# Grouped convolution ahead of a windowed attention: unstacked convolution for the first two images, one transfer per 32 channels, and a reordered preparation stage

## The chip, the cores and the metric

One core of a Trainium2 chip runs the kernel. The metric is the time of one execution on the device in microseconds (us), lower is better. TensorE is the matrix engine (PE in the profile, PEld its weight loads), VectorE is DVE, ScalarE is ACT, GpSimd is POOL, and SyncE (SP) only issues transfers. ScalarE and GpSimd issue transfers too, so SPq and ACTq in a row mean the transfer-issuing side of those engines.

## The reference, cut to what matters

The input is 16 images of 28 x 28 positions and 128 channels, all in float32. Two residual blocks follow each other:

```python
x = x + conv3x3(group_norm(x), W)          # 32 groups of 4 channels, "SAME" padding
x = x + neighborhood_attention(group_norm(x), w_qkv, b_qkv, rpb, w_proj, b_proj)
```

`group_norm` takes its statistics over all positions of an image and 4 channels. The convolution has 32 groups of 4 channels, so an output channel reads only the 4 input channels of its group. The attention has 16 heads of 8 dimensions, each query looks at a 7 x 7 window of keys, and a learned table `rpb` of 13 x 13 entries per head is added to the logits by relative position.

## The kernel before, in words

Channels lie on the 128 partitions, positions along the free dimension. The program is written engine by engine, with the order on each engine written out by hand and semaphores between them. It has two stages.

**The preparation stage** (up to about 242 us) runs over 32 **slots** `h`, two per image, each for 14 of the 28 rows (392 positions) of image `m = h // 2`. It loads the images in natural layout, turns each to channels-on-partitions on TensorE (`turn_input`, L1336, seven 112 x 112 transposes, four in the first half of the slot and three in the second), keeps them by ScalarE (`keep_input`, L807) and takes their statistics on VectorE (`input_stats`, L1052). The statistics of four images at a time go through a chain of small steps on VectorE, TensorE and ScalarE (`CHAINS`, L379). VectorE writes the normalized image into a zero-bordered buffer `padded[m % 2]` (`pad_image`, L1107). Then the convolution of that image can run (`convolve`, L1365), in two forms:

- **Unstacked**, for image 0 only: nine matmuls per slot, one per tap of the 3 x 3 filter, each with a 128 x 128 weight `wconv` that is zero outside the 4 x 4 group blocks. The moving operand is `padded` itself, shifted by the tap. `wconv` is loaded by GpSimd's queue (L689) and masked by VectorE (L1246).
- **Stacked**, for images 1 to 15: for each block `t` of 32 channels three copies of the padded image, shifted by 0, 1 and 2 columns, are put on top of each other on 96 partitions. One matmul with a 96 x 32 weight `wstack` then handles three taps of 32 channels, and the four blocks `t` write four different quarters of the output partitions. A slot takes 3 filter rows x 4 blocks = 12 such matmuls. The copies are transfers from SBUF to SBUF (`copy_image`, L473), three per block, twelve per image: SyncE issues those of blocks 0 and 1, ScalarE those of blocks 2 and 3, in slot `2m - 2`, once `pad_image(m)` is done.

VectorE adds the convolution to the image (`add_conv`, L1110), and takes the statistics of the second norm (`output_stats`, L1116). Beside the convolution each slot prepares the attention. In slots 3 to 16 TensorE picks the position biases from the table, two **units** a slot, each 24 or 32 small matmuls (`pick_unit`, L1401), and VectorE keeps them in three additions each (`keep_unit`, L1140). In slots 17 to 24 two **patches** a slot are rounded by VectorE (`round_patch`, L1158, in the slot ahead), turned by TensorE (`turn_patch`, L1419) and placed by VectorE (`place_patches`, L1170). In slots 18 to 20 the first image is projected to keys, queries and values (`project_qkv`, L1391); ScalarE takes the results from PSUM (`keep_qkv`, L848). In slots 20, 22 and 24 SyncE stores them in parts to DRAM, in slot 25 it loads them back in the layout of the scores (`fill_queries`, `fill_keys`), and in slots 26 to 28 the first maxima are computed.

The order of a slot on TensorE is in L1523 to L1559: the small sums of a statistics chain, the first part of the next image's transposes, the first unit, the patches, the projections, filter rows 0 and 1, the rest of the transposes, the second unit, filter row 2. TensorE may start slot `h` when `add_conv(h - 2)` is done and, for stacked images, the copies of image `m` have landed:

```python
pe.wait_ge(s[f"copies_in{m % 2}"], 192 * ((m + 1) // 2))
pe.wait_ge(s["wstack_ready"], 3)
```

The order of a slot on SyncE is in L605 to L627, on ScalarE in L971 to L998, on VectorE in L1250 to L1291. SyncE's queue is strictly in order, and some of its entries wait for others' work: `store_keys` for ScalarE and GpSimd, `fill_queries` for all stores to have landed (`wait(sp, "q_stored", ...)`, L545), `move_maxima` for VectorE.

**The attention stage** (from about 242 us to the end) runs 32 chunks (half images) of 16 tiles each: scores, bias, exponential, weighting, selection, projection. The change does not touch its code.

## Time and profile before

| | us |
|---|---|
| median of 3 runs | 1065.13 |
| lowest and highest of these | 1064.41, 1065.50 |
| the profiled execution | 1068.84 |
| its span, first to last instruction | 1066.8 |
| preparation stage in it | 0 to 242 |
| attention stage in it | 242 to 1066.8 |
| mean granted TensorE clock | 0.87 of full |

The profiled execution is 3.71 us above the median and 2.04 us longer than its span. The page cuts the span into 40 slices and gives for each engine the busy share, and for TensorE the granted clock in tenths of full speed. The full speed is 2.4 GHz, and 0.5 stands for 1.2 GHz. The timeline view lists instructions with start and duration and, in brackets, how long the engine sat idle before them and what released it. The chain of waits follows the end of the program back from step to step.

### The profile page before, as it was taken

What the parts mean: (1) busy time and instruction counts of PE and PEld (TensorE: products, weight loads), DVE (VectorE), ACT (ScalarE), POOL (GpSimd) and SP (SyncE); (2) the same over time, 40 slices, a digit from 0 to 9 for tenths busy, and PEclk for the clock granted to TensorE, in tenths of its full rate; (3) what the DMA queues carried; (4) which work ended last, traced back from release to release, by engine and by line L of the source; (5) the groups of instructions that cost most, each with busy time, mean ns of one, the idle gap of its engine ahead of it and who ended that gap; (6) DMA issues with size and microseconds to landing.
All of it is one profiled execution on the core that took longest, in us unless ns stands there. A gap on an engine that the chain in (4) does not pass through costs nothing.

```text
span 1066.8 us, 41868 instructions
## 1 busy us (share of the span) xinstructions
PE 952.5 (89%) x16669; PEld 630.3 (59%) x16669; DVE 822.3 (77%) x2117; ACT 642.4 (60%) x1808; POOL 484.6 (45%) x847
## 2 busy tenths in 40 slices
PE   4899997777899999999999999989999999999985
PEld 3455542235666666666676666656666666666763
DVE  4377876755879787887888787868897878788875
ACT  2111033205687868787777767666878686868653
POOL 7000002324474746464655555554647474646431
PEclk9755557678999989999899889998999898999997
DMA  9955555965555657474756465746665665737331
GB/s 233 218 161 134 136 135 148 285 185 172 165 152 167 192 142 202 118 227 103 215 144 203 117 191 143 209 118 186 163 180 155 166 186 147 205 99 226 104 87 39
DMA packets 131136, 175.00 MB, mean 164 GB/s; under 512 B 33624, under 2 KB 109944, under 8 KB 127616
## 3 DMA queue, kind: packets, MB, share of 16 engines
q1 hardware_dynamic: 125056, 157.94, 54.3%
q10 hardware_dynamic: 4608, 10.35, 3.8%
q0 software_dynamic: 1280, 4.05, 1.3%
q8 instruction: 133, 2.18, 0.9%
q14 instruction: 59, 0.48, 0.2%
HBM read 83.64 MB, written 67.55 MB: 142 GB/s over the span
## 4 chain that ended last, share of the span: by engine, by line
PE 64%; DVE 13%; issue 8%; ACT 7%; DMA 4%; ACTq 2%; SPq 2%; POOL 0%; DVEq 0%
PE PS L1453 14%; PE PS L1492 10%; PE PS L1476 8%; PE PS L1381 7%; PE PS L1398 6%; PE PS L1469 6%; PE PS L1435 5%; DVE area L1187 3%; DVE S L1208 3%; ACT area L845 3%; PE PS L1415 3%; ACT S L937 2%; DVE masked L1219 2%; PE PS L1502 2%; PE PS L1346 1%
## 5 line engine op out<-in xcount | busy, mean ns | idle before, releaser
L727 POOL TENSOR_TENSOR late<-masked 128x48 f32<-128x48 f32 (+1 forms) x512 | 152.6, 299 | 371.0 <-DVE masked L1219 359.7
L937 ACT ACTIVATE S<-S 128x384 f32<-128x384 f32 (+1 forms) x512 | 282.4, 554 | 25.2 <-DVE S L1208 21.8
L1208 DVE TENSOR_TENSOR S<-PS,bias 128x384 f32<-128x384 f32 (+1 forms) x512 | 282.4, 552 | 2.5 <-PE PS L1453 0.4
L1453 PE MATMUL PS<-area 97*128 97x48 bf16 (+1 forms) x4096 | 250.2, 208 | 37.9 <-DVE S L1208 32.7
L1198 DVE TENSOR_REDUCE mcol<-PS 128x6 bf16<-128x480 f32 (+2 forms) x288 | 176.1, 612 | 128.6 <-PE PS L1476 128.4
L930 ACT ACTIVATE VT<-PS 128x128 f32<-128x128 f32 x448 | 131.9, 294 | 182.6 <-PE PS L1435 179.2
L1453 PEld LDWEIGHTS PS<-area 97*128 97x128 bf16 x4096 | 179.0, 103 | 85.3 <-DVE S L1208 40.7
L1492 PE MATMUL PS<-S,VT 128*18 128x48 f32 x8192 | 197.0, 215 | 6.5 <-issue 5.9
L1492 PEld LDWEIGHTS PS<-S,VT 128*18 128x18 f32 x8192 | 117.4, 100 | 133.1 <-issue 66.2
L1476 PEld LDWEIGHTS PS<-area 128*128 128x128 bf16 x1568 | 144.9, 156 | 23.0 <-issue 8.7
L1435 PE MATMUL PS<-cst,area 128*128 128x128 f32 x448 | 141.9, 317 | 12.5 <-ACT VT L930 11.6
L1219 DVE TENSOR_TENSOR masked<-PS,cst 128x96 f32<-128x96 f32 (+1 forms) x512 | 128.2, 250 | 27.7 <-PE PS L1492 25.8
L1476 PE MATMUL PS<-area 128*128 128x80 bf16 x1568 | 142.0, 228 | 2.2 <-issue 2.2
L845 ACT ACTIVATE area<-PS,bqkv 128x224 f32<-128x224 f32 (+5 forms) x384 | 113.4, 424 | 31.4 <-issue 18.2
L1187 DVE TENSOR_SCALAR area<-area,cst 128x392 bf16<-128x392 bf16 x320 | 122.7, 413 | 0.0
L767 POOL TENSOR_SCALAR area<-area,cst 128x392 bf16<-128x392 bf16 x80 | 105.7, 1322 | 29.8 <-PE PS L1476 29.8
L1469 PE MATMUL PS<-biasp,identb 128*128 128x480 bf16 (+2 forms) x288 | 108.0, 375 | 2.5 <-issue 1.3
L1381 PE MATMUL PS<-area,wstack 96*32 96x392 f32 x468 | 96.3, 823 | 3.6 <-DMA area<-padded 3.6
L760 POOL TENSOR_TENSOR area<-area 128x336 bf16<-128x336 f32 (+1 forms) x96 | 94.3, 984 | 9.1 <-ACT area L910 9.1
L747 POOL TENSOR_TENSOR area<-area 128x336 f32<-128x336 f32 (+1 forms) x96 | 82.7, 863 | 10.9 <-ACT area L901 10.9
L1435 PEld LDWEIGHTS PS<-cst,area 128*128 128x128 f32 x448 | 67.6, 151 | 16.8 <-ACT VT L930 8.6
L920 ACT ACTIVATE area<-area,cst 128x392 bf16<-128x392 bf16 x112 | 72.4, 652 | 0.0
(102 smaller groups left out, 1017.9 us busy)
## 6 DMA issues: line engine op xcount, KB each, us to landing
area<-k_parts SPq DMA_DIRECT2D x32, 1008.0 KB, 7.1
...
```

What stands on the lines that cost most here:

```text
L727: nc.gpsimd.tensor_tensor(sel[:, c % SEL_RING, :, :, t0:t0 + count], m[:, :, 0], m[:, :, 1], ALU.add).then_inc(s["summed"], 1)
L937: nc.scalar.activation(S[:, n % 4, 0:cols], S[:, n % 4, 0:cols], ACT.Exp).then_inc(s["probs"], 1)
L1187: last = nc.vector.tensor_scalar(Qbd[:, h, :, :], qparts[0].rearrange("p (a q t) -> p a q t", a=2, q=PATCH)[:, c % 2], cst[:, C_HEAD + h:C ...
L1198: nc.vector.tensor_reduce(out=mcol[:, first:first + count], in_=PS[:, PEAK, 0:PATCH_KEYS * count].rearrange("p (t k) -> p t k", k=PATCH_KEYS),
L1208: nc.vector.tensor_tensor(S[:, n % 4, 0:cols], PS[:, SCORE + n % 2, 0:cols], bias[:, at:at + cols], ALU.add).then_inc(s["biased"], 1)
L1219: nc.vector.tensor_tensor(masked[:, n % 2, 0:4 * q].rearrange("p (g h q) -> p g h q", g=2, h=GROUP_HEADS), src, mask, ALU.mult).then_inc(s ...
L1381: last = mm(to[32 * t:32 * t + 32, :], wstack[0:96, row, 32 * t:32 * t + 32], image[:, first:first + HALF_ROWS, 0:SIDE], start=row == 0, s ...
L1435: nc.tensor.transpose(PS[:, VALUE, 0:128], V[c // 2 % 2][:, key:key + 128], ident).then_inc(s["value_in"], 1)
L1453: last = mm(PS[:, SCORE + n % 2, cols * g:cols * (g + 1)], key_rows[a][0:PEAK_ROW + 1, g, key:key + 128], query_rows[a][0:PEAK_ROW + 1, :, ...
L1469: mm(PS[:, PEAK, 0:PATCH_KEYS * count], identb[:, :], biasp[:, a, table_first:table_first + count, :], start=True, stop=False)
L1476: last = mm(PS[:, PEAK, PATCH_KEYS * i:PATCH_KEYS * (i + 1)], queries[:, :, first + i], rows[:, :, col:col + MIDDLE_W], start=False, stop= ...
L1492: last = mm(PS[32 * (g % 4):32 * (g % 4) + VALUE_COLS, SUM + n % 2, at:at + q], VT[:, w % 4, g, :], S[:, n % 4, q * g:q * (g + 1)], start= ...
```

## The change

- **Unstacked for two images.** `stacked(m)` is true for images 2 to 15. Image 1 is now convolved with nine 128 x 128 matmuls per slot from `padded[1]`, like image 0, and needs no copies.
- **One transfer per block.** `copy_tiles` copies a block of 32 channels in one transfer with an overlapping source pattern (32 partitions x 3 shifts x 898), to 96 partitions. The rows of the stack are now interleaved (channel, shift), and `wstack` is laid out to match: its loads go to every third partition, and its mask is one multiplication of 96 partitions instead of three of 32. An image takes four transfers instead of twelve.
- **Who issues them.** Up to image 12 SyncE issues two and ScalarE two, as before. For images 13 to 15 (slots 24, 26, 28) ScalarE issues all four and SyncE none.
- **Small loads moved.** ScalarE's 16 loads of `bqkv` move from the program's start to slots 5, 7, 9 and 11, four in each, and the scaling of `bqkv` and the copy of the weights to slot 13.
- **Filter weights.** The unstacked `wconv` is loaded in four transfers instead of nine, and its masking on VectorE moves from behind the padding of images 0 and 1 to ahead of `inverse_roots(0)`.
- **Patches later.** `turn_patch` moves on TensorE from ahead of filter row 0 to between filter rows 1 and 2.

```diff
@@ -167,7 +167,7 @@
-C_ID, C_GROUP, C_HEAD, C_OUT, C_SUM, CONSTS = 0, 128, 256, 272, 274, 402
+C_ID, C_GROUP, C_HEAD, C_OUT, C_STACK, C_SUM, CONSTS = 0, 128, 256, 272, 274, 306, 434
@@ -183,6 +183,8 @@
...
     c[:, C_HEAD:C_HEAD + HEADS] = (p % HEADS)[:, None] == np.arange(HEADS)[None]
+    stacked = p[:96] // 3
+    c[:96, C_STACK:C_STACK + 32] = stacked[:, None] // NORM_GROUP == np.arange(32)[None] // NORM_GROUP
     head_of_row = np.where(p % 32 < GROUP_DIMS, p % 32 // HEAD_DIM, 0)
@@ -304,7 +306,8 @@
...
-        FIRST_LATE = 10
+        FIRST_STACKED, LAST_STACKED = 2, 15
+        FIRST_LATE, FIRST_BY_SCALAR = 10, 13
         COPY, SPAN = PAD * PAD, PAD * PAD - 2
@@ -378,6 +381,7 @@
...
         STATS_BANK, TURN_BANK, LAST_STATS_BANK = SUM, SUM + 1, MISC + 1
+        BIAS_LOADS = {5: (0, 1), 7: (2, 3), 9: (4, 5), 11: (6, 7)}
         FIRST_PEAKS = {26: (0, 1, 2), 27: (3, 4, 5), 28: (6, 7, 8)}
@@ -470,10 +474,15 @@
...
-        def copy_image(eng, m, tiles):
...
+        def stacked(m):
+            return FIRST_STACKED <= m <= LAST_STACKED
...
+        def copy_tiles(eng, m, tiles):
...
+            if not stacked(m):
+                return
             eng.wait_ge(s["padded_ready"], m + 1)
-            if m > 2:
+            if m > FIRST_STACKED + 1:
                 eng.wait_ge(s["conv"], 2 * m - 2)
@@ -481,9 +490,9 @@
...
             for t in tiles:
-                for dc in range(3):
-                    eng.dma_start(copies(m)[t][32 * dc:32 * dc + 32, 0:SPAN], padded[m % 2][32 * t:32 * t + 32, dc:dc + SPAN]
-                                  ).then_inc(s[f"copies_in{m % 2}"], 16)
+                block_of = padded[m % 2][32 * t:32 * t + 32, 0:SPAN]
+                shifts = bass.AP(block_of.tensor, block_of.offset, [list(block_of.ap[0]), [1, 3], [1, SPAN]])
+                eng.dma_start(copies(m)[t][0:96, 0:SPAN], shifts).then_inc(s[f"copies_in{m % 2}"], 16)
@@ -603,8 +612,8 @@
...
             for h in range(SLOTS):
-                if h % 2 == 0 and h // 2 + 1 < IMAGES:
-                    copy_image(sp, h // 2 + 1, range(0, 2))
+                if h % 2 == 0 and h // 2 + 1 < FIRST_BY_SCALAR:
+                    copy_tiles(sp, h // 2 + 1, range(0, 2))
                 if 2 * X_RING + h < IMAGES:
@@ -685,17 +694,17 @@
...
             pool.wait_ge(s["cleared"], 1)
-            for tap in range(9):
-                pool.dma_start(wconv[:, tap, :], conv_w[tap // 3, tap % 3].unsqueeze(0).broadcast_to([CH // NORM_GROUP, NORM_GROUP, CH])
-                               ).then_inc(s["wconv_in"], 16)
+            for i in range(NORM_GROUP):
+                taps = conv_w[:, :, i, :].rearrange("r t o -> (r t) o").unsqueeze(0).broadcast_to([CH // NORM_GROUP, 9, CH])
+                pool.dma_start(wconv[i:CH:NORM_GROUP, :, :], taps).then_inc(s["wconv_in"], 16)
             for i in range(2):
...
                 pool.dma_start(table[i], rows.rearrange("h a b -> (a b) h"), allow_slow_non_contiguous=True).then_inc(s["table_in"], 16)
-            for dc in range(3):
-                for dr in range(3):
-                    pool.dma_start(wstack[32 * dc:32 * dc + 32, dr, :], conv_w[dr, dc].unsqueeze(0).broadcast_to([8, NORM_GROUP, CH])
-                                   ).then_inc(s["wstack_in"], 16)
+            for dr in range(3):
+                for dc in range(3):
+                    taps = conv_w[dr, dc].unsqueeze(0).broadcast_to([32 // NORM_GROUP, NORM_GROUP, CH])
+                    pool.dma_start(wstack[dc:96:3, dr, :], taps).then_inc(s["wstack_in"], 16)
             for i in range(2):
@@ -818,23 +827,26 @@
...
-            for which in range(2):
-                of = b_qkv[CH * which:CH * (which + 1)].rearrange("(g l d o) -> d l g o", l=2, d=HEAD_DIM, o=1)
-                for d in range(HEAD_DIM):
+            def load_biases(d):
...
+                for which in range(2):
+                    of = b_qkv[CH * which:CH * (which + 1)].rearrange("(g l d o) -> d l g o", l=2, d=HEAD_DIM, o=1)
                     act.dma_start(bqkv[HEADS * d:HEADS * (d + 1), which:which + 1], of[d], allow_slow_non_contiguous=True
                                   ).then_inc(s["loaded"], 16)
...
+            def prepare_weights():
...
+                act.wait_ge(s["loaded"], SMALL_LOADS)
+                nc.scalar.mul(bqkv[:, 0:1], bqkv[:, 0:1], SCALE).then_inc(s["weights"], 1)
+                for which in range(2):
+                    nc.scalar.activation(wqk[:, which, :].rearrange("p (d l g) -> p l d g", l=2, d=HEAD_DIM),
+                                         wqkv[:, CH * which:CH * (which + 1)].rearrange("p (g l d) -> p l d g", l=2, d=HEAD_DIM),
+                                         ACT.Copy).then_inc(s["weights"], 1)
...
             for i in range(X_RING):
...
             root(0)
-            act.wait_ge(s["loaded"], SMALL_LOADS)
-            nc.scalar.mul(bqkv[:, 0:1], bqkv[:, 0:1], SCALE).then_inc(s["weights"], 1)
...
-            for which in range(2):
-                nc.scalar.activation(wqk[:, which, :].rearrange("p (d l g) -> p l d g", l=2, d=HEAD_DIM),
-                                     wqkv[:, CH * which:CH * (which + 1)].rearrange("p (g l d) -> p l d g", l=2, d=HEAD_DIM),
-                                     ACT.Copy).then_inc(s["weights"], 1)
...
             def misc(k):
@@ -974,8 +986,15 @@
...
                         keep_input(TURN_FROM + h, side)
-                    if h % 2 == 0 and h // 2 + 1 < IMAGES:
-                        copy_image(act, h // 2 + 1, range(2 + side, 3 + side))
+                    if h % 2 == 0 and h // 2 + 1 < FIRST_BY_SCALAR:
+                        copy_tiles(act, h // 2 + 1, range(2 + side, 3 + side))
+                if h % 2 == 0 and FIRST_BY_SCALAR <= h // 2 + 1 < IMAGES:
+                    copy_tiles(act, h // 2 + 1, range(4))
+                if h in BIAS_LOADS:
+                    for d in BIAS_LOADS[h]:
+                        load_biases(d)
+                if h == 13:
+                    prepare_weights()
                 if h == 14:
@@ -1238,13 +1257,13 @@
...
             spreads_of_groups(0)
+            dve.wait_ge(s["wconv_in"], 16 * NORM_GROUP)
+            nc.vector.tensor_tensor(wconv[:, :, :], wconv[:, :, :], group.unsqueeze(1).broadcast_to([128, 9, CH]), ALU.mult
+                                    ).then_inc(s["wconv_ready"], 1)
             inverse_roots(0)
...
                 pad_image(i)
-            dve.wait_ge(s["wconv_in"], 16 * 9)
-            nc.vector.tensor_tensor(wconv[:, :, :], wconv[:, :, :], group.unsqueeze(1).broadcast_to([128, 9, CH]), ALU.mult
-                                    ).then_inc(s["wconv_ready"], 1)
             split_table()
@@ -1252,11 +1271,9 @@
...
                     dve.wait_ge(s["wstack_in"], 16 * 9)
-                    for dc in range(3):
-                        rows = slice(32 * dc, 32 * dc + 32)
-                        own = wstack[rows, :, :].rearrange("p r (t o) -> p (r t) o", o=32)
-                        nc.vector.tensor_tensor(own, own, group[rows, rows].unsqueeze(1).broadcast_to([32, 12, 32]), ALU.mult
-                                                ).then_inc(s["wstack_ready"], 1)
+                    blocks = wstack[0:96, :, :].rearrange("p r (t o) -> p (r t) o", o=32)
+                    own = cst[0:96, C_STACK:C_STACK + 32].unsqueeze(1).broadcast_to([96, 12, 32])
+                    nc.vector.tensor_tensor(blocks, blocks, own, ALU.mult).then_inc(s["wstack_ready"], 1)
                 for k in chain_at(h, 1):
@@ -1367,21 +1384,21 @@
...
                 if row == 0:
-                    if m:
-                        pe.wait_ge(s[f"copies_in{m % 2}"], 192 * ((m + 1) // 2))
-                        pe.wait_ge(s["wstack_ready"], 3)
+                    if stacked(m):
+                        pe.wait_ge(s[f"copies_in{m % 2}"], 64 * (m // 2))
+                        pe.wait_ge(s["wstack_ready"], 1)
                     else:
-                        pe.wait_ge(s["padded_ready"], 1)
+                        pe.wait_ge(s["padded_ready"], m + 1)
                         pe.wait_ge(s["wconv_ready"], 1)
...
                         pe.wait_ge(s["conv_added"], h - 1)
-                if m:
+                if stacked(m):
                     for t in range(4):
...
                 else:
-                    image = padded[m].rearrange("p (r c) -> p r c", c=PAD)
+                    image = padded[m % 2].rearrange("p (r c) -> p r c", c=PAD)
                     for c in range(3):
@@ -1529,8 +1546,6 @@
...
                     pick_unit(units[0])
-                for k in patches_at(h):
-                    turn_patch(k)
                 for at in (h, h + 0.5):
@@ -1552,6 +1567,8 @@
...
                     patch_scores(0, peaks[1])
+                for k in patches_at(h):
+                    turn_patch(k)
                 convolve(h, 2)
```

The rows below are of the instruction order on an engine as the program gives it (line, operation, tiles, shape, repeats). TensorE, slots 1 to 3, from the middle of slot 1 to the first transposes of slot 3, before:

```order
L1346 MATMUL PS<-cst,area 128x112 x3
L1386 MATMUL PS<-padded,wconv 128x392 x3
L1346 MATMUL PS<-cst,area 128x112 x4
L1381 MATMUL PS<-area,wstack 32x392 x8
L1346 MATMUL PS<-cst,area 128x112 x3
L1381 MATMUL PS<-area,wstack 32x392 x4
L1346 MATMUL PS<-cst,area 128x112 x4
```

and now:

```order
L1363 MATMUL PS<-cst,area 128x112 x3
L1403 MATMUL PS<-padded,wconv 128x392 x3
L1363 MATMUL PS<-cst,area 128x112 x4
L1403 MATMUL PS<-padded,wconv 128x392 x6
L1363 MATMUL PS<-cst,area 128x112 x3
L1403 MATMUL PS<-padded,wconv 128x392 x3
L1363 MATMUL PS<-cst,area 128x112 x4
```

The 12 stacked matmuls of slot 2 (`area,wstack`) have become 9 unstacked ones (`padded,wconv`). The nine of slot 3 change in the same way, and slot 4 is the first stacked one.

TensorE, slots 20 and 21 (`late,wstack` is the convolution, `identb,S` are the patches), before:

```order
L1381 MATMUL PS<-late,wstack 32x392 x12
L1360 MATMUL PS<-small,cst 128x4
L1426 MATMUL PS<-identb,S 128x128 x2
L1381 MATMUL PS<-late,wstack 32x392 x12
L1426 MATMUL PS<-identb,S 128x128 x2
L1381 MATMUL PS<-chosen,wstack 32x392 x3
```

and now:

```order
L1398 MATMUL PS<-late,wstack 32x392 x8
L1443 MATMUL PS<-identb,S 128x128 x2
L1398 MATMUL PS<-late,wstack 32x392 x4
L1377 MATMUL PS<-small,cst 128x4
L1398 MATMUL PS<-late,wstack 32x392 x8
L1443 MATMUL PS<-identb,S 128x128 x2
L1398 MATMUL PS<-late,wstack 32x392 x4
```

The two patches stood ahead of all 12 convolution matmuls of their slot, and now stand behind the first 8.

SyncE's queue, from slot 24 to slot 28 (`late<-padded` and `chosen<-padded` are copies for the stacks, `area<-q_parts` and `area<-k_parts` the loads back in slot 25, `area<-mcol` the maxima), before:

```order
L485 DMA chosen<-padded 32x898 x6
L510 DMA x_mid<-area 128x784
L530 DMA k_parts<-area 128x672 x2
L530 DMA q_parts<-area 128x392 x2
L547 DMA area<-q_parts 48x3136 x2
L556 DMA area<-k_parts 96x5376
L485 DMA late<-padded 32x898 x6
L510 DMA x_mid<-area 128x784
L566 DMA area<-mcol 1x128x24
L566 DMA area<-mcol 1x128x18
L485 DMA chosen<-padded 32x898 x6
```

and now:

```order
L519 DMA x_mid<-area 128x784
L539 DMA k_parts<-area 128x672 x2
L539 DMA q_parts<-area 128x392 x2
L556 DMA area<-q_parts 48x3136 x2
L565 DMA area<-k_parts 96x5376
L519 DMA x_mid<-area 128x784
L575 DMA area<-mcol 1x128x24
L575 DMA area<-mcol 1x128x18
L519 DMA x_mid<-area 128x784
```

The copies of images 13, 14 and 15 are gone from this queue. They stood behind the loads back (image 14) and behind the second maxima (image 15).

## Rows read from the trace of the kernel before

**Rows 1.** Busy time by stage (us, us busy and count by engine, clock, DMA share, GB/s).

```profile
43.50:120.00 76.50, 76.50 (x754) 41.36 (x754) 54.22 (x118) 9.80 (x21) 0.80 (x1) 0.50 0.58 152
120.00:156.00 36.00, 35.94 (x395) 16.71 (x392) 30.71 (x72) 6.52 (x3) 0.43 (x1) 0.50 0.53 132
156.00:242.00 86.00, 65.25 (x458) 22.72 (x458) 52.68 (x167) 18.09 (x45) 24.61 (x21) 0.71 0.73 199
242.00:1066.00 824.00, 750.59 (x14979) 533.84 (x14979) 667.26 (x1704) 598.35 (x1720) 437.68 (x786) 0.93 0.57 159
```

**Rows 2.** Timeline of the first 30 us: start, duration, engine, instruction, idle before.

```profile
2.22 9.64 ACTq L824 DMA_DIRECT2D bqkv<-b_qkv  x15
...
13.57 1.57 PE L1346 MATMUL PS<-cst,area 112*128 112x112 f32 x7 [2.32 <-ACT area L811]
...
19.39 0.16 DVE L1089 TENSOR_SCALAR small<-PS 128x4 f32<-128x4 f32 x1 [0.74 <-PE PS L1360]
...
20.91 1.73 DVE L1101 TENSOR_SCALAR padded<-area,small 128x784 f32<-128x784 f32 x2
...
21.59 1.01 PE L1346 MATMUL PS<-cst,area 112*128 112x112 f32 x4 [2.23 <-DMA area<-x]
...
22.56 1.35 DVE L1246 TENSOR_TENSOR wconv<-wconv,cst 128x1152 f32<-128x1152 f32 x1
...
24.05 6.20 PE L1386 MATMUL PS<-padded,wconv 128*128 128x392 f32 x11 [1.46 <-DVE wconv L1246]
```

**Rows 3.** Timeline of TensorE, slots 1 and 2.

```profile
33.08 4.13 PE L1386 MATMUL PS<-padded,wconv 128*128 128x392 f32 x12
...
43.50 2.84 PE L1381 MATMUL PS<-area,wstack 96*32 96x392 f32 x16 [3.62 <-DMA area<-padded]
```

**Rows 4.** Chain of waits, slots 3 to 5: start, duration, what.

```profile
54.95 1.46 PE PS L1381 x8
...
58.31 2.77 PE PS L1381 x16
...
61.84 0.96 PE PS L1415 x24
...
66.59 2.77 PE PS L1381 x16
```

**Rows 5.** Timeline of TensorE, slots 20 and 21.

```profile
176.03 2.18 PE L1381 MATMUL PS<-late,wstack 96*32 96x392 f32 x24
...
182.04 0.38 PE L1426 MATMUL PS<-identb,S 128*128 128x128 bf16 x2 [3.51 <-DVE S L1167]
182.35 4.15 PE L1381 MATMUL PS<-late,wstack 96*32 96x392 f32 x24
```

**Rows 6.** The 3 us before the clock fell in slot 30.

```profile
234.00:237.00 3.00, 1.43 (x17) 0.55 (x17) 2.83 (x8) 0.00 (x0) 3.00 (x3) 1.00 0.72 215
```

**Rows 7.** Timeline of ScalarE, slot 20.

```profile
184.13 2.00 ACT L845 ACTIVATE area<-PS,bqkv 128x224 f32<-128x224 f32 x6 [8.68 <-issue]
```

**Rows 8.** Timeline of VectorE, slots 21, 26 and 28.

```profile
186.32 0.18 DVE L1094 RECIPROCAL small<-small 128x4 f32<-128x4 f32 x1 [3.64 <-ACT small L819]
...
204.65 0.69 DVE L1101 TENSOR_SCALAR padded<-area,small 128x784 f32<-128x784 f32 x1
...
223.72 0.69 DVE L1101 TENSOR_SCALAR padded<-area,small 128x784 f32<-128x784 f32 x1
```

**Rows 9.** Timeline of TensorE, the first matmuls of slots 26, 28 and 30.

```profile
209.15 0.88 PE L1381 MATMUL PS<-chosen,wstack 96*32 96x392 f32 x3 [5.04 <-DMA area<-padded]
...
226.65 1.54 PE L1381 MATMUL PS<-late,wstack 96*32 96x392 f32 x8 [5.34 <-DMA late<-padded]
...
236.01 0.53 PE L1381 MATMUL PS<-chosen,wstack 96*32 96x392 f32 x3 [1.57 <-DMA chosen<-padded]
```

**Rows 10.** Timeline of SyncE's DMA queue, slots 26 and 28.

```profile
215.08 4.95 SPq L485 DMA_DIRECT2D late<-padded  x6
...
230.42 3.74 SPq L485 DMA_DIRECT2D chosen<-padded  x6
```

## The prediction

> **What bounds the kernel now.** I read the page's slices first: the granted clock is low in the first quarter of the span and nowhere else for long. The stage table places it. From 43.5 to 156 us TensorE is busy all the time at clock 0.50, from 156 to 242 us it is busy 65.25 of 86.00 us at 0.71, and the attention stage runs at 0.93 [rows 1]. The change leaves the attention stage alone, so I carry its 824 us over and ask when it starts. Three regimes come before it.
>
> First the start. ScalarE's queue issues `bqkv` loads until 11.86 us. The convolution begins at 24.05 us, behind the padding (from 20.91 us) and the masking of `wconv` (22.56 us, 1.35 us) [rows 2].
>
> Then the slots with table units. TensorE sat idle 3.62 us for the copies of image 1 [rows 3] and went on at 1.2 GHz, where it stayed although it hardly paused again until 156 us [rows 1]. One slot is the step from 58.31 to 66.59 us, about 8.2 us [rows 4]. TensorE bounds it, since VectorE is busy only 54.22 of 76.50 us [rows 1].
>
> Last the slots with patches, 156 to 242 us. There TensorE waits in turn for VectorE (3.51 us before the patches of slot 21 [rows 5]), for ScalarE through VectorE [rows 7, 8], and for copies: 5.0, 5.3 and 1.6 us before images 13, 14 and 15 [rows 9].
>
> **The change, part by part.** *Start.* TensorE's last wait before turning image 3, 2.32 us, is put down to ScalarE [rows 2], and without the 16 issues ScalarE could begin sooner. But ScalarE's first two keeps, begun at 11.9 us behind its issues, take about 0.5 us each and are done at 12.9 us, and TensorE went on at 13.57 us, so I think image 3 itself was late, and take 0 (bounds 0 and -2.3 us). The masking now lies where VectorE stood 0.74 us for the variance sum, until 19.39 us [rows 2]. It takes 1.35 us from 18.65 us on, so everything behind it is 0.6 us later. The first padded image is ready at 20.91 + 0.6 + 0.87 (half of 1.73) = 22.4 us. TensorE must also turn image 4 first, from 21.59 us for 1.01 us [rows 2], until 22.6 us. Convolution at 22.65 instead of 24.05 us: **-1.4 us**. If image 4's load lands later, because the big table loads start 2 us earlier behind four `wconv` transfers in place of nine, this goes to 0 or +1.
>
> *Slots 2 and 3, unstacked.* Twelve records of unstacked matmuls took 4.13 us at full clock [rows 3], so 18 records, a slot, take 6.2 us, or 5.9 us start to start. Transposes add 1.0 us a slot, the units of slot 3 (0.96 us each at half clock [rows 4]) about 0.7 us each. Slot 2 takes 6.9 us and slot 3 8.3 us. The convolution of slot 2 could begin at 43.50 - 3.62 = 39.9 us before, 15.8 us after that of slot 0, so now at 38.5 us. Filter row 2 of slot 3 then ends at 38.5 + 6.9 + 8.3 - 0.55 (slot 2's first transposes lie ahead of 38.5) = 53.15 us. Before it ended at 54.95 + 1.46 = 56.41 us [rows 4]. That is -3.3 us in all, **-1.9 us** for the two slots: 3.6 us of waiting goes, and full clock pays for most of the additional columns.
>
> *Slots 4 and 5.* The clock arrives here at 2.4 GHz, since nothing has paused TensorE. 24 records of stacked matmuls take 2.18 us at full and 4.15 us at half clock [rows 5], so a slot at full clock is 8.2 - 2.0 (convolution) - 0.8 (transposes) - 0.7 (units) = 4.7 us. But VectorE needs 54.22 / 76.50 of 8.2 = 5.8 us for an average slot, 6.5 us with its small waits: TensorE would now pause for it. I expect the clock to fall in slot 4 or 5. The reason is slot 30, where it fell at 237 us after 3 us with 1.43 us of work [rows 6]. Slot 4 saves between 0 (falls at once) and 3.5 us, slot 5 between 0 and 2.4 us, held by VectorE. I take **-4.0 us**, the upper half, since slot 4 itself has no pause. From slot 6 to 16 TensorE is back at 8.2 us a slot: nothing.
>
> A rule of the Trainium skill speaks for more. TensorE: Matmul & The Clock Gate, section "The HAM clock gate (the "warmup" mystery)", says that the engine goes back to half rate only after it was idle for a whole window. By that the clock would stay up in these slots, and the sum would be about 16 us lower. The trace speaks against it: before 237 us TensorE was idle for only about half of the stretch [rows 6].
>
> *The other moves up to slot 16* cost nothing: four `bqkv` issues of 0.6 us (9.64 us for 15 [rows 2]) in a slot where ScalarE is busy 9.80 of 76.50 us [rows 1], and one masking of `wstack` in place of three. Their cover is TensorE's 8.2 us; without it they would cost 2.5 us in each of four slots. Four transfers of three times the size move the same bytes. No row shows such a pattern, but the copies of a steady image have two slots, 16 us, to land, so at half to twice their speed nothing changes there.
>
> *Patches.* In slots 17 and 18 TensorE and VectorE wait for the normalized first image; 0.4 us at best. In slot 21 filter rows 0 and 1 can run in the 3.51 us for which TensorE stood before the patches [rows 5]. ScalarE issued six copies in slot 20, without other work for 8.68 us, then took the values from 184.13 us on [rows 7], and only then the square root for which VectorE stood 3.64 us [rows 8]. With two issues it is there some 3 us earlier. So both loops shorten by about 3.5 us, and the copies of image 11 are issued sooner too. What is late next is VectorE's placing, since the patches are turned 1.5 to 3 us later in a slot. I take **-3.0 us** (0 to -5).
>
> *Copies of images 13 to 15.* Image 13: SyncE's six issues become four on ScalarE, 1 us sooner, but SyncE's stores now compete: **-0.5 us** (+2 to -3). Image 14: padded at 205.3 us [rows 8], yet SyncE came to its six copies only at 215.08 us [rows 10], held by its wait for the stores, and they had landed 6.6 us after the last issue, at 226.65 us [rows 9]. ScalarE's four would be out by 208 us and land, even at 9 us, before TensorE wants them (226.65 - 5.34 = 221.3 us). Image 15: padded at 224.4 us, issued by SyncE from 230.42 to 234.16 us [rows 8, 10]. ScalarE's last is out at 227 us and lands at 231 us; before, slot 30 began at 236.01 us. So the two together give **-5.0 us**, not 5.3 + 1.6, the end being set by image 15's copies. The bounds are 0 (the loads back fill the transfer engines) and -7.
>
> *Sum.* -1.4 - 1.9 - 4.0 - 3.0 - 0.5 - 5.0 = -15.8 us. The profiled execution of 1068.84 us becomes 1053.0 us. It lies 3.7 us above the median, so the median goes from 1065.13 to **1049.3 us**. A change within 0.2% (2.1 us) can't be told from none.
>
> **The rivals.** *The clock stays at 2.4 GHz up to slot 16.* Then VectorE bounds the slots. Seven slots at 6.5 in place of 8.2 us and four at 5.8 in place of 6.8 us (VectorE is busy 30.71 of 36.00 us there [rows 1]) give 16 us more: 1033 us. For it: in slot 20 twelve stacked matmuls ran at full clock without a fall [rows 5]. Against: rows 6, and that each slot would have a pause of 2 us.
>
> *The transfers are the bound in slots 22 to 30.* The transfer engines are busy 0.73 of this stage [rows 1]. If ScalarE's copies share them with the stores and loads back that now start earlier, the last two terms go and half of the patches': 1049.3 + 5.5 + 1.5 = 1056.3 us.
>
> *Slower: the unstacked slots run at 1.2 GHz.* Nine unstacked matmuls then take 11.8 us, twice 5.9. Slot 2 lasts 13.5 and slot 3 15.4 us, and filter row 2 of slot 3 ends near 67 us, 10.5 us later than before instead of 3.3 us earlier. The -4.0 us of slots 4 and 5 does not come, and with half of the later terms (-4.3 us) the median is 1065.1 + 10.5 - 4.3 = 1071.3 us. It decides from one pause of TensorE of about 2 us between slots 0 and 2 on, if image 4, 5 or 6 lands late. For it: TensorE did wait 2.23 us for image 4 [rows 2]. Against: it waited for no other image, and the copies of image 1 no longer compete.
>
> *The change doesn't reach the end*: what is won before 156 us is lost again in waits on something with its own clock. Every wait that I followed in this stage leads back to a slot, so this gets little: 1065 us.
>
> **How the numbers follow.** My forecast 0.56, full clock 0.14, transfers bound 0.20, slower 0.06, nothing 0.04. The first three are faster, 0.90; 0.01 of it goes to the slower side for terms that turn out against me together. The range has to leave out 0.2: it goes from 1036, which cuts off most of the full-clock case, to 1058 us, which holds the transfer case and cuts off the last two.
>
> **What would show it.** Right: slot 2 begins without a wait at clock 1.00, and filter row 2 of slot 3 ends near 53 us; the clock falls in slot 4 or 5 and slots 6 to 11 last 8.2 us; no wait over 2 us before the patches; the wait before image 14 is gone; the attention stage starts near 226 us. Wrong: clock 1.00 at 100 us (first rival), waits for copies of over 3 us after slot 22 (second), an unstacked slot of 12 us (third), or an attention stage that is not 824 us long.

## The result, and the profile after

The change made the kernel faster by 9.2 us: 1055.17 us median (1050.38 to 1059.82, 13 runs), against 1064.41 us (1058.66 to 1066.8, 13 runs) for the kernel before, run in turn with it on one chip. The ratio is 0.9921, 95% interval 0.9901 to 0.9941. I had forecast 15.8 us. The profiled execution took 1055.17 us, its span is 1053.4 us. Some executions of a kernel take over 1.5% longer than its fastest one, and all medians and ratios in this document leave them out.

The stages of the new kernel, cut as in [rows 1] (the columns are those of that group):

```profile
43.50:120.00 76.50, 74.36 (x815) 40.61 (x814) 63.98 (x144) 9.54 (x22) 1.22 (x1) 0.63 0.62 164
120.00:156.00 36.00, 35.65 (x338) 15.21 (x338) 26.91 (x76) 12.95 (x16) 2.75 (x2) 0.56 0.49 131
156.00:242.00 86.00, 64.19 (x567) 25.49 (x559) 48.65 (x166) 22.10 (x63) 25.81 (x25) 0.74 0.79 224
```

TensorE is at a mean clock of 0.63 instead of 0.50 in the first stretch, and VectorE does 63.98 us of work in it instead of 54.22. More slots fit into it. The transfer engines are busier between 156 and 242 us, 0.79 instead of 0.73.

The start, from the timeline (the rows answer to [rows 2]):

```profile
5.99 1.01 ACT L820 ACTIVATE area<-PS 128x448 f32<-128x448 f32 x2 [3.76 <-PE PS L1363]
...
11.70 1.57 PE L1363 MATMUL PS<-cst,area 112*128 112x112 f32 x7 [0.71 <-DMA area<-x]
...
16.70 1.35 DVE L1261 TENSOR_TENSOR wconv<-wconv,cst 128x1152 f32<-128x1152 f32 x1
...
19.34 1.01 PE L1363 MATMUL PS<-cst,area 112*128 112x112 f32 x4 [1.85 <-DMA area<-x]
...
20.30 6.61 PE L1403 MATMUL PS<-padded,wconv 128*128 128x392 f32 x12
```

ScalarE's first eviction is at 5.99 us, image 3 is turned at 11.70 instead of 13.57 us, and the convolution begins at 20.30 instead of 24.05 us, 3.75 us earlier. It begins when the first transposes of image 4 are done, and these had waited for the image itself (1.85 us).

Slots 3 to 8 in the chain of waits (answering to [rows 4]):

```profile
48.38 2.08 PE PS L1403 x6
...
54.50 0.64 DVE bias L1171
...
70.97 2.77 PE PS L1398 x16
...
79.14 2.77 PE PS L1398 x16
...
87.74 2.77 PE PS L1398 x16
```

Filter row 2 of slot 3 ends at 50.46 us (before: 56.41 us). Then the chain leaves TensorE and runs through VectorE, whose shares of the bias table (L1171) set the pace until slot 7, at 70.97 us. From there on a slot is TensorE's again and takes 8.2 to 8.6 us. The clock fell at 62.7 us, in slot 5. Of the windows around the fall, the middle one holds TensorE's longest pause of the 8 us before it, 0.97 us:

```profile
56.00:59.00 3.00, 3.00 (x67) 1.92 (x64) 2.83 (x9) 0.49 (x2) 0.00 (x0) 1.00 1.00 252
59.00:62.00 3.00, 2.03 (x34) 1.15 (x30) 2.93 (x6) 0.01 (x1) 0.00 (x0) 1.00 1.11 346
62.00:66.00 4.00, 4.00 (x49) 2.01 (x46) 3.42 (x12) 0.64 (x2) 0.00 (x0) 0.59 0.59 120
```

What TensorE waited for in the slots with patches (us in total, times, longest), first the kernel before, 156 to 242 us:

```profile
PE PS L1426 <- DVE S L1167: 7.2, 5, 3.5
PE PS L1381 <- DMA late<-padded: 5.3, 1, 5.3
PE PS L1381 <- DMA area<-padded: 5.0, 1, 5.0
PE PS L1381 <- DMA chosen<-padded: 1.6, 1, 1.6
```

and the changed kernel, 144 to 226 us:

```profile
PE PS L1398 <- DMA area<-padded: 11.3, 3, 5.4
...
PE PS L1443 <- DVE S L1186: 1.9, 1, 1.9
```

The wait before the patches (L1426, now L1443) shrank from 7.2 to 1.9 us and the one before image 14 is gone. The waits for copies are as long as before in sum, 11.3 us against 11.9. They now stand before images 11, 13 and 15:

```profile
171.34 0.87 PE L1398 MATMUL PS<-chosen,wstack 96*32 96x392 f32 x3 [3.99 <-DMA area<-padded]
...
194.62 0.87 PE L1398 MATMUL PS<-chosen,wstack 96*32 96x392 f32 x3 [5.39 <-DMA area<-padded]
...
219.52 0.88 PE L1398 MATMUL PS<-chosen,wstack 96*32 96x392 f32 x3 [1.93 <-DMA area<-padded]
```

Image 13's copies leave ScalarE's queue late and then take 8.18 us to land. The queue (timeline of ScalarE), then the transfer's piece of the chain of waits:

```profile
182.17 4.19 ACTq L495 DMA_DIRECT2D chosen<-padded  x3
186.39 2.34 ACTq L495 DMA_DIRECT2D area<-padded  x1
```

```profile
186.39 8.18 DMA area<-padded
```

Four issues took 6.5 us here. Where less moves, two take 1.22 us on SyncE's queue and 1.92 us on ScalarE's (their timelines):

```profile
111.44 1.22 SPq L495 DMA_DIRECT2D area<-padded  x2
```

```profile
111.45 1.92 ACTq L495 DMA_DIRECT2D area<-padded  x2
```

The page's list of transfers (count, KB each, median us from issue to landing) has for the copies, before and then after:

```profile
area<-padded ACTq DMA_DIRECT2D x63, 112.2 KB, 3.9
```

```profile
area<-padded ACTq DMA_DIRECT2D x19, 336.8 KB, 6.4
```

So a single transfer lands later than one of its three predecessors did, and the three together had more issues ahead of them.

Slot 17 shows what fewer issues are worth on ScalarE. Behind its copies of image 9 it has an activation of 4.68 us and then the square root that VectorE's normalization of the first image waits for. The kernel before (timelines of ScalarE and VectorE):

```profile
150.26 4.01 ACTq L485 DMA_DIRECT2D area<-padded  x6
154.36 4.68 ACT L968 ACTIVATE area<-cst 1x5376 bf16<-1x5376 f32 x1 [7.62 <-issue]
159.37 0.18 DVE L1094 RECIPROCAL small<-small 128x4 f32<-128x4 f32 x1 [2.50 <-ACT small L819]
```

and the changed one:

```profile
138.51 1.91 ACTq L495 DMA_DIRECT2D area<-padded  x2
140.52 4.68 ACT L980 ACTIVATE area<-cst 1x5376 bf16<-1x5376 f32 x1 [7.68 <-issue]
145.53 0.18 DVE L1113 RECIPROCAL small<-small 128x4 f32<-128x4 f32 x1 [0.40 <-ACT small L828]
```

VectorE's wait fell from 2.50 to 0.40 us, and the add of slot 17 now follows that of slot 16 after 4.4 instead of 7.4 us.

### The profile page after: what moved, and what is told of

Read it like the earlier page. It is cut to its first block, busy times and chain, and to the rows that moved or that the text cites. A ratio compares the mean times of both kernels' runs of the same rounds, so it can differ in the third digit from the quotient of the medians.

```text
span 1053.4 us, 41704 instructions
## 1 busy us (share of the span) xinstructions
PE 947.1 (90%) x16657; PEld 628.7 (60%) x16657; DVE 813.7 (77%) x2115; ACT 643.7 (61%) x1808; POOL 484.7 (46%) x842
## 4 chain that ended last, share of the span: by engine, by line
PE 65%; DVE 13%; ACT 8%; issue 7%; DMA 4%; SPq 1%; ACTq 1%; POOL 0%; DVEq 0%; POOLq 0%
PE PS L1470 14%; PE PS L1509 10%; PE PS L1493 8%; PE PS L1415 7%; PE PS L1398 6%; PE PS L1486 6%; PE PS L1452 5%; ACT area L857 3%; DVE area L1206 3%; DVE S L1227 3%; PE PS L1403 3%; ACT S L949 2%; DMA area<-padded 2%; PE PS L1432 2%; DVE masked L1238 2%
## 5 line engine op out<-in xcount | busy, mean ns | idle before, releaser
L1470 PE MATMUL PS<-area 97*128 97x48 bf16 (+1 forms) x4096 | 250.7, 208 | 40.3 <-DVE S L1227 36.5
L1470 PEld LDWEIGHTS PS<-area 97*128 97x128 bf16 x4096 | 179.2, 103 | 90.5 <-DVE S L1227 46.4
L1238 DVE TENSOR_TENSOR masked<-PS,cst 128x96 f32<-128x96 f32 (+1 forms) x512 | 128.4, 251 | 30.7 <-PE PS L1509 29.8
L1206 DVE TENSOR_SCALAR area<-area,cst 128x392 bf16<-128x392 bf16 x320 | 119.9, 405 | 0.0
L1398 PE MATMUL PS<-area,wstack 96*32 96x392 f32 x420 | 82.6, 763 | 0.0
## 6 DMA issues: line engine op xcount, KB each, us to landing
area<-padded ACTq DMA_DIRECT2D x19, 336.8 KB, 6.4
```

What stands on the lines that cost most here:

```text
L1206: last = nc.vector.tensor_scalar(Qbd[:, h, :, :], qparts[0].rearrange("p (a q t) -> p a q t", a=2, q=PATCH)[:, c % 2], cst[:, C_HEAD + h:C ...
L1238: nc.vector.tensor_tensor(masked[:, n % 2, 0:4 * q].rearrange("p (g h q) -> p g h q", g=2, h=GROUP_HEADS), src, mask, ALU.mult).then_inc(s ...
L1398: last = mm(to[32 * t:32 * t + 32, :], wstack[0:96, row, 32 * t:32 * t + 32], image[:, first:first + HALF_ROWS, 0:SIDE], start=row == 0, s ...
L1470: last = mm(PS[:, SCORE + n % 2, cols * g:cols * (g + 1)], key_rows[a][0:PEAK_ROW + 1, g, key:key + 128], query_rows[a][0:PEAK_ROW + 1, :, ...
```

## The experiments

I had two questions: how much each part of the change is worth, and why slots 6 to 16 stayed slow. To see parts of a few us I read four marks in every profile: VectorE's add at the end of slot 0 and of slot 16 (L1133), the first scores of the attention stage (L1470), and the end of the span. All are in us. "Before here" is the median of the kernel before in the same session. The ratios are those on record with their intervals; they are not the quotients of the two medians. There were four sessions (the given pair, then the rows from again_before, from again_after2 and from three_transfers on), each on one chip.

| kernel | median (runs) | before here | ratio, interval | add of slot 0 | slot 0 to 16 | slot 16 to first scores | attention |
|---|---|---|---|---|---|---|---|
| before (given) | | | | 32.9 | 123.3 | 86.3 | 824.3 |
| changed (given) | 1055.17 (13) | 1064.41 | 0.9921, 0.9901-0.9941 | 29.2 | 115.3 | 81.6 | 827.3 |
| again_before | 1065.98 (8) | 1059.85 | 1.0062, 1.0020-1.0103 | 33.5 | 120.0 | 86.8 | 820.9 |
| again_after | 1056.56 (6) | 1059.85 | 0.9960, 0.9933-0.9987 | 27.2 | 115.3 | 83.5 | 824.7 |
| stack_image1 | 1061.18 (10) | 1059.85 | 1.0020, 0.9983-1.0057 | 28.7 | 125.5 | 87.7 | 825.6 |
| mixed16 | 1049.22 (4) | 1059.85 | 0.9870, 0.9826-0.9914 | 40.5 | 105.8 | 86.6 | 817.9 |
| again_after2 | 1057.40 (10) | 1063.37 | 0.9908, 0.9870-0.9947 | 29.8 | 115.3 | 81.7 | 828.0 |
| tables_held | 1057.97 (8) | 1063.37 | 0.9952, 0.9913-0.9992 | 28.0 | 115.3 | 86.7 | 828.8 |
| mixed16_held | 1051.87 (4) | 1063.37 | 0.9882, 0.9838-0.9927 | 28.6 | 107.3 | 84.5 | 830.8 |
| sync_copies | 1062.29 (10) | 1063.37 | 1.0015, 0.9969-1.0060 | 29.5 | 115.3 | 87.9 | 829.8 |
| three_transfers | 1062.50 (12) | 1066.62 | 0.9975, 0.9939-1.0011 | 28.8 | 115.2 | 97.6 | 826.1 |
| early_patches | 1053.60 (6) | 1066.62 | 0.9852, 0.9805-0.9898 | 28.6 | 115.3 | 80.4 | 824.3 |
| biases_first | 1056.09 (7) | 1066.62 | 0.9899, 0.9859-0.9939 | 30.6 | 115.3 | 87.4 | 825.8 |
| mixed31 | 1047.68 (6) | 1066.62 | 0.9797, 0.9752-0.9842 | 28.5 | 105.6 | 88.0 | 823.8 |

**again_before and again_after**, the two kernels unchanged.

> The kernel before once more, for how much the two stages vary by themselves. If the preparation stage is steady, its first attention matmul starts within 1 us of 248.4 us, and the scatter of the whole time (1058.7 to 1066.8 us) comes from the attention stage, which took 818.4 us in the first profile and would lie some us below that here. If the preparation stage scatters, the start itself moves by several us, and then the 16.8 us between the two profiled kernels is partly luck.

> The changed kernel once more. Theory: the preparation stage ends near 231.6 us again (within 1 us), and the clock falls in slot 5 near 62.5 us. Rival: the end scatters by 3 to 5 us with the moment at which the clock falls, since that moment is not tied to the program.

The kernel before came out at 1.0062 against itself, with an interval that leaves out 1. So the intervals are too narrow here, and I take no difference under 0.6% (6 us) between two ratios for shown by the times alone. Where I claim less, a stage length in the table has to carry it. again_after2 was a third look:

> The changed kernel once more, for the spread of its start and beside the next ones on the same chip. In two profiles its first convolution was added at 27.2 and 29.2 us; in the kernel with the mixed third row, whose start is the same program, at 40.5 us, because image 4 landed 12 us late behind the table loads. Theory: the start falls into either kind from one execution to the next (here anything from 27 to 41 us), and this is why the medians differ by 7 to 9 us while the profiles differ by 14 to 16 us. Rival: 40.5 us was a single accident, and the start is 27 to 30 us again.

Its rival held: the add of slot 0 came at 29.8 us. The three measurements of the changed kernel give 0.9921, 0.9960 and 0.9908. In all three the attention stage starts within 1 us of 226 us and the clock falls in slot 5 (at 62.7, 60.0 and 63.8 us). The kernel before isn't as steady: its first scores came at 242.5 and then 240.3 us. In the changed kernel the stage from slot 0 to slot 16 repeats to 0.1 us. The stage after it does not: tables_held and biases_first run the same instructions there and took 86.7 and 87.4 us, where the changed kernel took 81.6, 83.5 and 81.7.

**stack_image1** stacks image 1 again (slots 2 and 3) and keeps everything else of the change.

```diff
-        FIRST_STACKED, LAST_STACKED = 2, 15
+        FIRST_STACKED, LAST_STACKED = 1, 15
```

> The changed kernel with image 1 stacked again. Theory (the clock): TensorE waits some 3 to 4 us for the copies in slot 2 and the clock falls there, so slots 2 to 5 run at 1.2 GHz; slot 7 starts near 79 us instead of 71.0 us, and the attention stage starts 7 to 8 us later than in the changed kernel. Rival (start and transfers): the gain up to slot 7 came from the earlier start and the fewer transfers, and slot 7 moves by no more than 2 us.

The timeline of TensorE and the stretch behind it:

```profile
37.81 0.71 PE L1363 MATMUL PS<-cst,area 112*128 112x112 f32 x4 [2.53 <-DMA area<-x]
41.46 2.84 PE L1398 MATMUL PS<-area,wstack 96*32 96x392 f32 x16 [2.94 <-DMA area<-padded]
```

```profile
38.00:50.00 12.00, 9.06 (x71) 3.87 (x74) 3.27 (x7) 1.54 (x3) 0.00 (x0) 0.51 0.96 204
```

The wait for the copies is back, the clock fell at 38.2 us instead of 62.7, and slots 0 to 16 took 125.5 instead of 115.3 us. The median is 4.6 us above again_after's, which is at the limit of what I take for shown by the times; the stage length carries it. The add of slot 7 comes 9.7 us later (8 us in the theory). The unstacked image 1 is the heart of the change: with it TensorE has no pause over 0.1 us from 20.30 to 55.48 us, in slot 4. The 10.2 us of the profile are more than it is worth as a rule. The profiled execution took 1069.37 us, 8.2 us above the median, the image turned in slot 1 came late too (2.53 us), and the copies landed 11.5 us after their issue. Against again_before, whose wait was 1.64 us, slots 0 to 16 are 5 us shorter in the changed kernel. Adds 0 to 3 took 20.66 us there and take 21.25 us here, so the unstacked slots are no shorter than stacked ones with a short wait. The gain is the clock that they hand on: adds 3 to 7 took 32.27 us and take 26.88 us.

**mixed16** adds to the change that filter row 2 of every image is convolved unstacked in slots 4 to 16 (three products on all 128 rows and columns, in place of four on 96 rows and 32 columns).

```diff
-                if stacked(m):
+                if stacked(m) and not (row == 2 and MIXED[0] <= h <= MIXED[1]):
...
+                elif stacked(m):
+                    image = padded[m % 2].rearrange("p (r c) -> p r c", c=PAD)
+                    for c in range(3):
+                        last = mm(to, wconv[:, 3 * row + c, :], image[:, first:first + HALF_ROWS, c:c + SIDE],
+                                  start=False, stop=c == 2)
```

> The changed kernel with filter row 2 unstacked in slots 4 to 16 (three 128 x 128 matmuls in place of four 96 x 32). Theory (the clock falls because stacked slots leave TensorE too little work while VectorE is awaited): with the denser third row the clock stays at 2.4 GHz, VectorE bounds the slots at about 6.5 us, slot 17 starts near 132 us instead of 144.2 us, and the time falls by about 12 us more. Rival (the clock falls with any pause of TensorE, however short): it falls in slot 5 as before, unstacked thirds then cost 3.9 in place of 1.4 us a slot, and the time rises by up to 13 x 2.5 = 32 us.

From 66 to 136 us, the changed kernel and then mixed16:

```profile
66.00:136.00 70.00, 69.21 (x731) 35.27 (x728) 57.83 (x129) 11.34 (x17) 1.22 (x1) 0.50 0.52 140
```

```profile
66.00:136.00 70.00, 61.60 (x841) 37.67 (x840) 66.43 (x152) 12.84 (x21) 1.22 (x1) 0.97 0.67 176
```

A filter row takes longer unstacked at the same clock (2.15 us against 0.87 us for a stacked one, both at 2.4 GHz in the changed kernel's trace), and still TensorE is less busy, since it runs at 2.4 GHz until 131.7 us. VectorE, busy 66.43 of 70 us, now bounds these slots. Slots 0 to 16 took 105.8 us, 9.5 less, and the median is 7.3 us below again_after's, not the 12 us of my theory. In this profile image 4 landed late, and the time was below both kernels all the same:

```profile
31.19 1.01 PE L1364 MATMUL PS<-cst,area 112*128 112x112 f32 x4 [12.75 <-DMA area<-x]
```

**tables_held and mixed16_held** test whether the large table loads, which GpSimd's queue now issues at 12.98 us, hold up image 4. GpSimd waits for the images first:

```diff
+            pool.wait_ge(s["xin_in0"], 32)
+            pool.wait_ge(s["xin_in1"], 32)
             for i in range(2):
                 pool.dma_start(chosen[i], select[i].bitcast(BF16)).then_inc(s["pool_loaded"], 16)
```

> The changed kernel, with GpSimd waiting for images 4 and 5 to land before it issues the two table loads of 1.5 MB each. Theory: image 4 lands before 20 us in every execution, the first convolution is added at 27 to 29 us, the table is still there before slot 3, and the median falls by 2 to 5 us against the changed kernel, with a smaller spread. Rival (no collision): the median stays within 1 us, or rises if the table comes too late for slot 3.

> Both edits: filter row 2 unstacked in slots 4 to 16, and the table loads held. The step from the first addition to that of slot 16 was 105.8 us with the mixed row and 115.3 us in the changed kernel, in both its profiles. Theory: the clock is 1.00 from slot 1 to beyond 120 us again, the step is 106 us within 2 us, and the attention stage starts near 220 us; the median is 8 to 12 us below the changed kernel's. Rival (the long clock of the first run was luck): the clock falls somewhere between 60 and 120 us and the step is 110 us or more.

Image 4 landed in time in both, and also in all the profiles without the hold but mixed16's. One case in ten profiles without the hold and none in two with it settles nothing. The medians of tables_held and again_after2 lie within 1 us, as the rival said. In mixed16_held, with image 4 in time, the first scores came at 220.4 us, the earliest of all, but the attention stage was the longest, and the median is 5.5 us below again_after2's, less than the 8 to 12 us expected. The clock was not at 2.4 GHz throughout: it fell at 71.1 us, behind a pause of 1.55 us, and again at 122.3 us. After the first fall it was back within 7 us, where in the changed kernel it stayed down from 62.7 to 151 us. So what the unstacked row brings is in part that the clock returns.

```profile
66.00:71.00 5.00, 3.45 (x48) 1.93 (x46) 4.86 (x10) 1.00 (x2) 0.00 (x0) 1.00 0.87 213
71.00:78.00 7.00, 7.00 (x47) 4.39 (x40) 5.51 (x11) 0.45 (x1) 0.00 (x0) 0.51 0.81 220
78.00:122.00 44.00, 39.08 (x567) 24.26 (x569) 41.76 (x98) 6.96 (x14) 1.22 (x1) 1.00 0.51 137
```

**sync_copies** gives half of the copies of images 13 to 15 back to SyncE.

```diff
-        FIRST_LATE, FIRST_BY_SCALAR = 10, 13
+        FIRST_LATE, FIRST_BY_SCALAR = 10, 16
```

> The changed kernel with SyncE issuing two of the four copies of images 13 to 15 again. My step was that taking them off SyncE's queue gives 5.5 us. Theory of the prediction: the wait before image 14 is back at 4 to 5 us and the step from the addition of slot 16 to the first score (81.6 and 83.5 us in the changed kernel) grows by about 5 us. Rival (the transfer engines, not the queue, bound these slots): the waits only change places, and the step stays within 2 us of 82.5 us.

SyncE's queue, the transfer in the chain of waits, and TensorE:

```profile
202.46 1.24 SPq L495 DMA_DIRECT2D late<-padded  x2
```

```profile
203.10 11.15 DMA late<-padded
```

```profile
214.30 1.54 PE L1398 MATMUL PS<-late,wstack 96*32 96x392 f32 x8 [8.34 <-DMA late<-padded]
```

The wait before image 14 returned, 8.34 us, for the reason I had given (SyncE comes to them behind its stores) and one more, a landing of 11.15 us. First scores came 5.9 us later than in again_after2, and the median is 4.9 us above it. The stage length alone (87.9 us) would not show this, since tables_held and biases_first have nearly the same; the ratios, 1.0015 and 0.9908, do.

**three_transfers** sends the copies in three transfers of 112.2 KB again.

```diff
-                block_of = padded[m % 2][32 * t:32 * t + 32, 0:SPAN]
-                shifts = bass.AP(block_of.tensor, block_of.offset, [list(block_of.ap[0]), [1, 3], [1, SPAN]])
-                eng.dma_start(copies(m)[t][0:96, 0:SPAN], shifts).then_inc(s[f"copies_in{m % 2}"], 16)
+                for dc in range(3):
+                    eng.dma_start(copies(m)[t][dc:96:3, 0:SPAN], padded[m % 2][32 * t:32 * t + 32, dc:dc + SPAN]
+                                  ).then_inc(s[f"copies_in{m % 2}"], 16)
```

> The changed kernel with its copies sent as before: three transfers of 112.2 KB per 32 channels, where it sends one of 336.8 KB. Theory T (fewer issues were the gain of slots 17 to 31): with twelve issues an image the wait before image 14 comes back and the waits before images 11, 13 and 15 grow; from the add of slot 16 to the first score 86 to 87 us as in the kernel before, where the changed kernel takes 81.6 to 83.5; time 3 to 5 us above the changed kernel, about 1061. Rival U (the same bytes land no sooner or later either way; a single transfer only changes how the landing is reported): stage length 81.5 to 83.5 us, waits of TensorE for the copies 9 to 12 us in all, time within 2 us of the changed kernel. Rival V (the large transfer hurts, each lands 6.4 us after its issue and the small one 3.8): waits for the copies fall to 5 us or less and the time by 3 us or more.

ScalarE's queue and TensorE's wait before image 13:

```profile
187.96 7.45 ACTq L494 DMA_DIRECT2D chosen<-padded  x9
195.44 2.19 ACTq L494 DMA_DIRECT2D area<-padded  x3
```

```profile
206.26 0.88 PE L1398 MATMUL PS<-chosen,wstack 96*32 96x392 f32 x3 [11.23 <-DMA area<-padded]
```

Theory T, and by more than it said: 97.6 us from slot 16 to the first scores, the wait before image 13 is 11.23 instead of 5.39 us, and the median is 6.4 us above that of biases_first in the same session. The twelve issues took 9.6 us in place of 6.5. VectorE's wait in slot 17 is back at 2.52 us, and the add of slot 17 comes 7.1 us after that of slot 16, where the kernel before has 7.4 and the changed one 4.4 us. The profiled execution took 1069.62 us, 7.1 us above the median, so its 97.6 us may well overstate the difference. Up to slot 16 the number of transfers changed nothing (115.2 us).

**early_patches** turns the patches ahead of filter row 0 again, as before the change.

```diff
                 if units:
                     pick_unit(units[0])
+                for k in patches_at(h):
+                    turn_patch(k)
```

> The changed kernel with the patches turned at the start of a slot, ahead of its first filter row, as before the change. Theory T (the move is worth what my prediction gave it, about 3 us): in slots 17 to 31 TensorE waits for VectorE before the patch turns by 1 to 2 us in several slots, first score 2 to 4 us later, time 2 to 4 us above the changed kernel. Rival U (the copies of images 11, 13 and 15 end the waits there, whatever stands ahead): the waits only change their name, those for the copies get shorter by what the waits before the patches take; first score within 1 us, time within 1.5 us.

TensorE's waits from 144 to 224 us:

```profile
PE PS L1398 <- DMA area<-padded: 8.6, 2, 6.6
PE PS L1443 <- DVE S L1186: 3.9, 2, 3.5
...
PE PS L1398 <- DMA late<-padded: 1.9, 1, 1.9
```

Rival U. The 3.5 us before the patches are back, and the wait for the copies of image 11 is gone with them, while those of image 12 now come 1.9 us late; copies and patches together cost 14.4 us against 13.2. The stage took 80.4 us, the shortest of all, and the ratio, 0.9852, is below all three of the changed kernel. The runs show no gain from the move.

**biases_first** puts the 16 loads of `bqkv` back ahead of ScalarE's first eviction.

> The changed kernel with the eight pairs of bias loads back ahead of ScalarE's first evictions. Theory T (the move gave the start its gain): ScalarE's first eviction starts behind 16 issues, near 8 to 10 us instead of 5.99; the add of slot 0 comes 2 to 4 us later than 27.2 to 29.8, and the time grows by 2 to 4 us. Rival U (image 4's landing sets the start): the table loads start later too, image 4 lands sooner, and the add of slot 0 stays at 28 to 30 us; time within 1.5 us. Rival V: the transfers of the biases had disturbed slots 5 to 11; then it is faster by more than 1 us.

```profile
12.01 3.23 ACT L820 ACTIVATE area<-PS 128x448 f32<-128x448 f32 x8 [9.78 <-PE PS L1362]
...
13.04 1.54 PE L1362 MATMUL PS<-cst,area 112*128 112x112 f32 x7 [1.75 <-ACT area L820]
...
22.16 2.33 PE L1402 MATMUL PS<-padded,wconv 128*128 128x392 f32 x3 [1.25 <-DVE padded L1119]
```

TensorE waits for ScalarE again before turning image 3, and the convolution begins at 22.16 us instead of 20.30. The add of slot 0 is 1.9 us later than the mean of the changed kernel's three profiles (28.7 us), and 0.8 us later than the latest of them. That is theory T at the lower end of its 2 to 4 us; the time cannot tell it from nothing.

**mixed31** extends the unstacked filter row to the last slot.

```diff
-        MIXED = (4, 16)
+        MIXED = (4, 31)
```

> The changed kernel with filter row 2 of every stacked image unstacked (full 128 rows, three products instead of one with 96 rows), in slots 4 to 31, not only to 16. Theory T (at the full clock a slot of slots 17 to 30 saves nothing, since VectorE and the transfers bound it): first score as with slots 4 to 16 alone, near 220 us where image 4 lands in time, time 1049 to 1052. Rival U (the copies come late in slots 17 to 31 and the extra products, which need no copy, only add work: 28 more slots x 4 products): first score 2 to 6 us later, time 1052 to 1057. Rival V (the clock stays full to the first score and the slots get shorter with it): first score near 214 us, time 1043 to 1046.

It has the lowest ratio of all, 0.9797, and is 5.9 us below early_patches in the same session. Slots 0 to 16 took 105.6 us, as in mixed16. The waits for copies fell to 8.2 us in all, but the stage behind slot 16 took 88.0 us, not less than elsewhere, so rival V is out. The first scores came at 222.1 us, nearest to theory T. The clock fell here too, at 71.0 and 108.6 us, and was back within 7 us each time. Whether it differs from mixed16 is open: they ran in different sessions. Of the versions here it is the one to use; with the patches turned early it was not tried.

## Why the prediction was right, and where it was off

The time lies in the range (1036 to 1058 us), on the forecast side of no change, and 5.9 us above the forecast.

| term of the sum | forecast | the two given profiles | mean of 3 profiles after less mean of 2 before |
|---|---|---|---|
| start (add of slot 0) | -1.4 | -3.7 | -4.4 |
| slots 2 and 3 (adds of slots 0 to 3) | -1.9 | -2.7 | -1.1 |
| slots 4 and 5, and VectorE's backlog from them (adds of slots 3 to 7) | -4.0 | -5.4 | -5.4 |
| from there to slot 16 (adds of slots 7 to 16) | 0 | 0.0 | 0.0 |
| slot 17 (adds of slots 16 to 17) | 0 | -3.0 | -3.0 |
| slots 18 to 31 | -8.5 | -1.7 | -1.3 |
| attention | 0 | +3.0 | +4.1 |
| sum, of the unrounded terms | -15.8 | -13.5 | -11.0 |

**Start: under-sized.** I took 0 for ScalarE, because its first keeps were done at 12.9 us and TensorE went on at 13.57, and concluded that image 3 itself was late. It was not: image 3 was turned at 11.70 us. The releaser that [rows 2] names was the right one, and biases_first brings it back. About 1.9 us of the start are ScalarE's, close to the bound of 2.3 that I had set aside. The rest would be the masking's, whose term was -1.4; no run takes that part back alone.

**Slots 2 and 3: right in mechanism.** Slot 2 begins without a wait at clock 1.00 and lasts 6.6 us (6.9 forecast). Row 2 of slot 3 ends at 50.46 us (53.15 forecast, 2.35 of the difference from the start). stack_image1 shows the cause. The wait of 3.62 us in [rows 3] was a long one, though: in again_before it was 1.64 us, and against that profile these slots gain nothing.

**Slots 4 and 5: right in mechanism, 1.4 us under-sized.** VectorE became the bound and TensorE paused for it. The clock fell in slot 5, after a stretch with 2.03 of 3.00 us of work; I had taken the step from slot 30 [rows 6]. By the rule of the Trainium skill that I weighed (TensorE: Matmul & The Clock Gate, "The HAM clock gate (the "warmup" mystery)") the clock should have stayed up. The trace disagrees: in the eight profiles in which image 1 is unstacked and filter row 2 of the later images is stacked, the clock fell in slot 5, and in none of them had TensorE paused for more than 0.97 us in the 8 us before.

**From there to slot 16: right.** 67.1 us before and after. The rival of the full clock didn't come by itself. The kernels with the unstacked filter row bring it about, with 8.0 to 9.7 us over slots 0 to 16 in place of the 16 that I had priced. Slots 7 to 16 took 58.4 us in mixed16, where 6.5 and 5.8 us a slot (five and four slots) would make 55.7, and part of slot 6's gain had come with the changed kernel already.

**Slots 17 to 31: over-sized**, -4.3 for -8.5 us, and even that within this stage's spread of 6 us. Three microseconds of it come in slot 17, which I had given "0.4 us at best" and left out of the sum. I had not seen that ScalarE's long activation and its square root stand behind the issues of image 9's copies; three_transfers brings that wait back, early_patches doesn't. So my three terms, -8.5 us, stand against only 1.3 to 1.7 us in slots 18 to 31. *Patches, -3.0:* this step failed. The wait went as I said (7.2 to 1.9 us), but the next in line was not VectorE's placing. It was the copies of image 11, which had caused no wait before and now caused one of 3.99 us. They are issued 18.3 to 19.6 us after the add of slot 16 in the changed kernel's three profiles and 18.0 us after it in early_patches, so the move did not bring them sooner. early_patches shows no gain. *Image 13, -0.5:* 5.0 became 5.39 us. *Images 14 and 15, -5.0:* sync_copies bears that term out (+5.9 us to the first scores, +4.9 us in the median when undone). My rival of the transfers as the bound described the rest: the engines are at 0.79, a landing takes 8 us where I had allowed 9 but only for image 14, and it named "waits for copies of over 3 us after slot 22" as its sign. The sign is there, once (5.39 us). That rival's 1056.3 us is nearer to 1055.17 than my 1049.3.

**The step to the median failed, and here luck had a part.** I carried the profile's 3.7 us above the median over unchanged. The changed kernel's profiled execution was its median. Span against span the gain is 13.4 us, most of the 15.8 forecast; the median gained 9.2. The profile of before held a longer wait in slot 2 and a worse clock in the attention stage (824.3 against 820.9 us in again_before) than the second profile of that kernel has (0.93 against 0.95 in the clock). So 3.7 us of the forecast rested on how one execution of the kernel before happened to lie.

**Attention: open.** I carried 824 us over. In the 14 profiles it takes from 817.9 to 830.8 us, with the same instructions, and the three of the changed kernel are longer than the two of before by 4.1 us. The images' outputs drift apart a little at a time, so no single wait shows. Whether an earlier start makes this stage longer can't be told: the four profiles whose first scores come after 240 us average 824.2 us, the six before 228 us 826.5 us, with a spread of 2 to 3 us in each group.
